# The sixteenth score found may give the threshold of an upward search, in a one-core decoder layer

## The reference, cut to what matters

```
scores = einsum('bhqd,bhkd->bhqk', qn, kn) / temp     # 16 heads of 32, 256 keys
kk = max(1, S // 4)                                   # 64 of 256
vals, idx = top_k(scores, kk)
w = softmax(vals)                                     # all other weights are 0
out = einsum('bhqk,bhkd->bhqd', attn, v)
```

## Time and profile before

| | before |
|---|---|
| median of 3 runs | 3458.11 us (3455.98 to 3460.54) |
| profiled execution, its own time | 3452.61 us |
| its span, first to last instruction | 3450.8 us |
| mean granted TensorE clock | 0.935 |
| TensorE busy | 2917.6 us (85%) |
| VectorE busy | 2918.5 us (85%) |
| ScalarE busy | 2135.9 us (62%) |
| GpSimd busy | 1669.9 us (48%) |

### The profile page before, as it was taken

One profiled execution on the slowest core, in us unless ns is written; L12 is line 12 of the kernel. 1 busy time (PEld: TensorE's weight loads), 2 busy tenths in 40 slices (PEclk: granted clock), 3 DMA queues, 4 the chain that ended last, 5 costly groups with the idle time before them and its releaser, 6 DMA issues. The chain is left out here.

```text
span 3450.8 us, 60452 instructions
## 1 busy us (share of the span) xinstructions
PE 2917.6 (85%) x16154; PEld 1602.4 (46%) x16154; DVE 2918.5 (85%) x10240; ACT 2135.9 (62%) x5970; POOL 1669.9 (48%) x2285
## 2 busy tenths in 40 slices
PE   6799989988988789888988899799978889889845
PEld 3454555544544344444444544455544444445423
DVE  3888989889888888888898898888988899888982
ACT  2676767666666556665665676566756666566641
POOL 4355545545544355344544455455534555445523
PEclk9899999999999899999999999899989999989977
DMA  6000000000000000000000000000000000000000
GB/s 210 7 17 23 23 23 20 23 5 23 23 23 20 4 23 23 22 20 5 23 23 23 23 20 21 7 23 23 23 20 4 23 23 23 23 20 17 4 16 13
DMA packets 43577, 80.46 MB, mean 23 GB/s; under 512 B 3787, under 2 KB 11979, under 8 KB 43059
## 3 DMA queue, kind: packets, MB, share of 16 engines
q1 hardware_dynamic: 41554, 69.18, 6.0%
q0 software_dynamic: 1504, 5.77, 0.5%
HBM read 58.16 MB, written 16.78 MB: 22 GB/s over the span
## 5 line engine op out<-in xcount | busy, mean ns | idle before, releaser
L517 POOL TENSOR_SCALAR probs<-probs,kept_inv 128x256 f32<-128x256 f32 x1024 | 486.9, 496 | 921.5 <-DVE kept_inv L1770 921.5
L1732 DVE SCALAR_TENSOR_TENSOR probs<-scores,threshold,probs 128x256 f32<-128x256 f32 x1006 | 440.2, 502 | 110.8 <-ACT probs L782 54.9
L807 ACT ACTIVATE probsT<-work_ps 128x512 f32<-128x512 f32 x512 | 291.4, 597 | 290.9 <-PE work_ps L1029 253.5
L1684 DVE TENSOR_SCALAR near<-scores,flip 128x256 int32<-128x256 int32 x1024 | 468.4, 526 | 3.4
L772 ACT ACTIVATE scores<-score_ps,neg_guess 128x256 f32<-128x256 f32 x1024 | 397.4, 484 | 99.4 <-DVE kept_inv L1770 90.2
L1029 PE MATMUL work_ps<-ident,probs 128*128 128x128 f32 x2072 | 325.9, 295 | 152.1 <-POOL probs L517 94.0
L792 ACT ACTIVATE near<-scores 128x256 f32<-128x256 f32 x1024 | 414.1, 423 | 21.6 <-DVE nearest L1700 19.8
L1696 DVE MATCH_REPLACE8 near<-nearest,near 128x256 f32<-128x256 f32 x1024 | 407.6, 411 | 0.0
L1692 DVE MAX8 nearest<-near 128x8 f32<-128x256 f32 x1024 | 358.6, 412 | 6.4 <-DVE near L1684 4.7
L1700 DVE MAX8 nearest<-near 128x8 f32<-128x256 f32 x1024 | 358.1, 414 | 0.0
L484 POOL TENSOR_TENSOR inv_norm<-sumsq,minus_half 128x32 f32<-128x32 f32 x64 | 351.4, 5491 | 5.3
(11 more groups left out here) (171 smaller groups left out, 5523.9 us busy)
## 6 DMA issues: line engine op xcount, KB each, us to landing
x_in<-in_x_dram SPq DMA_DIRECT2D x32, 512.0 KB, 4.0
x_res<-in_x_dram SPq DMA_DIRECT2D x32, 512.0 KB, 4.6
out_dram<-rows SPq DMA_DIRECT2D x32, 512.0 KB, 3.1
c_sb<-in_ctx_dram SPq DMA_DIRECT2D x32, 256.0 KB, 2.7
scores<-in_L_ffn_W_dram SPq DMA_DIRECT2D x6, 1024.0 KB, 5.8
near<-in_L_ffn_W_dram SPq DMA_DIRECT2D x2, 1024.0 KB, 9.8
w_q<-in_L_attn_Wq_dram POOLq DMA_DIRECT2D x1, 1024.0 KB, 9.1
w_k<-in_L_attn_Wk_dram POOLq DMA_DIRECT2D x1, 1024.0 KB, 11.0
```

Of the source, the lines that this page charges most:

```text
L517: pool.tensor_scalar(probs[:, s % 2, h, j], probs[:, s % 2, h, j], kept_inv[:, s % 2, n:n + 1], 1.0, ALU.mult, ALU.mult).then_inc(s_pr, 1)
L807: act.activation(probsT[:, h, 2 * a:2 * a + 2], W[BANK_TP[s][2 * h + a]][:].rearrange("p (h k n) -> p h k n", h=2, k=NT), ACT.Copy).then_i ...
L1684: last = dve.tensor_scalar(near[:, h, j].bitcast(I32), scores[:, r, h, j].bitcast(I32), flip[:, r, n:n + 1].bitcast(I32), None, ALU.bitwis ...
L1732: step.mark(dve.scalar_tensor_tensor(out=probs[:, r, h, j], in0=scores[:, r, h, j], scalar=threshold[:, r, k:k + 1], in1=probs[:, r, h, j] ...
```

## The change

The last of the sixteen constants in `ranks` is made by the same rule as the others, so that a threshold in the sixteenth place is marked and picked. The test for an unsure row also looks at `sign_sum`: where it is LAST_BELOW = 2 x (64 - 16) - 256 = -160, which is N = 48 and so the sixteenth place of a downward search, a count of 1 or more leaves the row unsure, as before. In an upward search the sixteenth place (N = 79) is accepted when the count is 1. (Scores that are not in the list and equal the sixteenth are no harm upward: the 64 highest are the same set of values. Downward they would be kept in excess.) The check is one scalar_tensor_tensor in the place of one tensor_scalar.

```
+        LAST_BELOW = float(2 * (KEEP - WINDOW) - S)
...
                 for n in range(WINDOW):
-                    last = pool.memset(ranks[:, n:n + 1], (2.0 * n + 1.0) ** 2 - MIDDLE ** 2 if n < WINDOW - 1 else 0.5)
+                    last = pool.memset(ranks[:, n:n + 1], (2.0 * n + 1.0) ** 2 - MIDDLE ** 2)
...
                 step.wait(step.mark(dve.tensor_reduce(n_same[:], same, AX.X, ALU.add)))
-                dve.tensor_scalar(unsure[:, r], n_same[:], 1.0, None, ALU.not_equal).then_inc(s_bad, 1)
+                dve.scalar_tensor_tensor(out=unsure[:, r], in0=sign_sum[:, r], scalar=LAST_BELOW, in1=n_same[:],
+                                         op0=ALU.not_equal, op1=ALU.not_equal).then_inc(s_bad, 1)
```

## The result

| | before | after |
|---|---|---|
| median of 4 runs | 3458.01 us | 3398.56 us (3394.36 to 3399.89) |
| profiled execution, its own time | 3452.61 us | 3399.39 us |
| its span | 3450.8 us | 3397.6 us |
| mean granted TensorE clock | 0.935 | 0.946 |

The ratio is 0.9826, with a 95% interval of 0.9809 to 0.9843. The changed kernel is 59.5 us faster by the medians. The forecast was 3402.1 us, 56 us less; the time lies in the range of 3391 to 3416.

What follows compares the result with a forecast made beforehand. The prediction took VectorE's striking of rare heads to lie on the path without slack. Profiled 3452.6 less 56 (five heads), everything else nothing, gave 3396.6; plus 5.5 to the median of runs, 3402.1 us, range 3391 to 3416.

Steps and rivals of the forecast that it cites:

- The cost of a struck head: A head with an unsure row, sent to keep_top's Else branch: VectorE's 8 striking rounds add 11.1 to 11.2 us.
- The number of heads: Heads struck only for a threshold at the sixteenth place above: five of 18 go, in five sets, gaining 56 us.
- The rival with another count: The chip's guess differs in last bits, so only four sets leave the Else branch: 3413.6 us, chance 0.05.
- The three heads that the positions don't explain: Struck heads (10,3,3), (11,0,7), (14,2,6), put down to equal scores at the threshold; the change leaves them alone.
- Constant and rank comparison cost nothing: Setup memset of `ranks` and the equality finding a row's rank: same instructions, no added time.
- the test costs nothing: New unsure check on VectorE, 128 times: taken as nothing, between -2.0 us and +15.1 us.
- the outcome is the old one: In the new unsure check, everywhere but N = 48 the first comparison gives 1 and the result is unchanged.
- rival C: TensorE takes the bound over, giving back only its 7.88 us wait per struck set: 39 us, 3419; chance 0.05.
- Clock given back: Each set leaving the striking also returns TensorE clock, as (20,2) does: nearer 67 us in sum; not adopted.
- rival E: The check's longer form between search and TensorE's count outweighs the gain, needing 0.44 us more each; chance 0.02.

Runs made afterwards that it cites:

- never_struck_2: Kernel before with a test that finds no row unsure, and the reciprocal ending a set taken of ones: 3256.52 us, ratio 0.9431.
- fewer_places: Kernel before with the fifteenth place out too (two constants are 0.5), 44 heads struck: 3741.99 us, ratio 1.0826.
- constant_only: Kernel before with only the sixteenth constant made a rank, the old unsure test kept: 3362.22 us, ratio 0.9734.
- check_only: Changed kernel with the sixteenth constant put back to 0.5, the new unsure test kept: 3415.97 us, ratio 0.9883.
- ties_let_through: Kernel before with a row unsure only where the count is 0, equal scores at the threshold let through: 3438.20 us, ratio 0.9947.
- zero_above: Changed kernel with 1e-30 added to the scores inside the sign operation, as a bias read from a tile: 3422.95 us, ratio 0.9908.
- form_only: Changed kernel with the sixteenth constant back at 0.5 and LAST_BELOW = 1000, so new test form, old outcome: 3452.61 us, ratio 0.9993.
- one_strike: Changed kernel with one strike in a turn of the inner striking loop instead of two, eight turns: 3420.15 us, ratio 0.9890.

## Why the prediction was right, point by point

**The cost of a struck head** was put at 11.1 to 11.2 us with no slack under it. Held: 10.9 by never_struck_2, 11.0 by fewer_places, 11.6 by constant_only, 11.2 to 11.4 in the periods. It is a mean: in the kernel before, the two heads struck between 748.8 and 864.5 cost 9.2 us each, the two between 1177.6 and 1299.5 cost 12.3. The change itself measured 59.5 / 5 = 11.9, with an interval of 10.9 to 13.2 from that of the ratio. The 3.5 us by which the forecast fell short are within that; of the profile, 55.7 us are in the five places where they were expected, and the remaining differences are of both signs and in periods that the change doesn't touch.

**The number of heads** was five, (9,1,7), (13,0,1), (16,0,3), (20,2,7) and (24,0,2). Held to the head: exactly these are missing after, and the other 13 are at their old places. The rival with another count is out. The same working gave 8 and 26 heads for constant_only and fewer_places ahead of their runs, and both were met. The three that went in check_only were not expected there, but they are the three that it has at the sixteenth place below.

**The three heads that the positions don't explain** were put down to equal scores at the threshold. This step was wrong for two of three. In (10,3,3) and (11,0,7) a score lies on the guess (2e-9 and 4e-9 in my numbers), its sign is 0, `sign_sum` is odd and equals no rank. I had the near-tie only for (14,2,6) and extended it to the others. That (14,2,6) has equal scores is shown by ties_let_through, that the other two have a score on the guess by zero_above. It didn't matter to the sum, since the change leaves both kinds alone.

**Constant and rank comparison cost nothing, the test costs nothing.** Held: the test by form_only, 0.9993; the constant by constant_only, where 8 heads gave 92.5 us and their own price is 90, so that no cost is left to see. By the rule of the Trainium skill (VectorE: DVE Perf Modes, "Why `tensor_tensor` can't do 2×_2P or 4×") the form with two tensor sources loses the faster mode. That doesn't decide at 8 elements: 169 ns against 176. The prediction's sentence that elsewhere "the outcome is the old one" is right only with the new constant; check_only showed it.

**TensorE taking over** (rival C): out. With VectorE's striking gone entirely the time fell by 197 us, where that rival allowed 134.

**Clock given back.** The set of (20,2) was charged with 2.7 us for the slower period behind it. The two periods fell by 12.8 us against 13.4, but to charge them both to the set was not sound. ties_let_through still strikes (20,2,7), and the period behind it takes 97.5 us at a granted clock of 0.95, the second line shown with that run; in form_only, which strikes it too, it is 98.4 at 0.94 (2241.8 to 2340.2). So the slower period is not a fixed price of striking that set. The forecast hardly hangs on it, since 56 was taken from the means. The other four gave 9.6 to 12.0, so a loss like that at every struck set, 67 us in sum, isn't seen.

**The slower case** (rival E) needed 0.44 us more in each test; it is 7 ns less.

## What to carry to other kernels

When a rare slow branch sits in the program of an engine on whose results the others wait, count its uses and multiply by its whole length: here the time was linear in the count from 0 to 44, about 11 us each. What sends the data there is a question of the inputs, not of the profile, and can be worked out beforehand; the trace then tells by order and place whether the working is right, and every use that it leaves unexplained deserves its own cause. Before adding an operand or a few instructions to the ordinary path to spare the rare one, price both by their counts: 1024 times 86 ns cost more than two struck heads. And whether a small saving in every ordinary set comes back has to be measured: of 17 us, 3 to 7 did.

## What the runs showed of the hardware that was not expected

A ScalarE operation on 128x256 takes 424 ns without and 510 ns with a bias read from a tile. A turn of VectorE's loop with its semaphore clear leaves it idle for 0.47 to 0.49 us in most cases. one_strike, with four turns more in each of 13 heads, was 22 us slower, 0.42 for each turn, while its ordinary sets were 9 us shorter. A score of exactly 0 counts as 0 in a sum of signs: adding 1e-30 ahead of the sign took the two heads (10,3,3) and (11,0,7) out of the striking, and no others. And TensorE's busy time for the same matmuls goes with the granted clock, which is lower in the kernels that strike more heads: 2034.83 us at a granted clock of 0.97 where nothing was struck, 2097.71 at 0.91 with 34 struck heads, in this stretch of fewer_places:

```profile
804.50:3412.60 2608.10, 2097.71 (x11549) 1148.82 (x11548) 2243.44 (x7896) 1525.54 (x4278) 1184.18 (x1610) 0.91 0.05 18
```
